# Four chained attention layers on one core: the counting and mean products are moved from ahead of the causal attention's first score products to behind them

## The reference

```
Q = relu(x @ Wq + bq); K = relu(ctx @ Wk + bk); V = relu(ctx @ Wv + bv)
key_masks = sign(abs(sum(K, axis=-1)))          # a key counts if its row of K isn't all zero
scores = where(key_masks == 0, NEG, Q_ K_^T / 4)
scores = where(tril == 0, NEG, scores)           # NEG = -2**32 + 1, not minus infinity
out = relu(softmax(scores) V_ @ Wo + bo) + x, then a norm over each row
```

## Time and profile before

| what | us |
|---|---|
| median of 3 runs | 1596.85 |
| the three runs | 1592.26, 1596.85, 6304.54 |
| the profiled execution, device time | 1590.74 |
| its span | 1588.9 |
| PE busy | 1426.6 (90%) |
| DVE busy | 864.6 (54%) |
| ACT busy | 716.6 (45%) |
| mean granted PE clock | 0.965 |

### The profile page before, as it was taken

The page is one execution under the profiler, slowest core; times in us unless marked ns, Lnnn a source line. Parts: engine busy times, 40 slices in busy tenths (PEclk is TensorE's granted clock), DMA queues, the critical chain, the costliest instruction groups (busy, mean ns, idle before and its releaser), DMA issues.

```text
span 1588.9 us, 23992 instructions
## 1 busy us (share of the span) xinstructions
PE 1426.6 (90%) x8204; PEld 713.9 (45%) x8232; DVE 864.6 (54%) x2099; ACT 716.6 (45%) x1177; POOL 263.6 (17%) x138
## 2 busy tenths in 40 slices
PE   5999898888999988888999998988899998988886
PEld 2336555423533654543443464553263355455334
DVE  2663565585266256567355536556636635655762
ACT  0663353455366234427446425352825632625462
POOL 1004131301100413220110213121011041303001
PEclk9999999989999989998999998998999999999898
DMA  9000404303200230540310031242031005043210
GB/s 339 22 1 12 102 1 91 70 14 113 68 1 7 38 70 1 99 75 1 126 55 1 8 62 45 38 86 51 1 127 54 1 8 106 2 71 64 41 60 14
DMA packets 44776, 85.28 MB, mean 54 GB/s; under 512 B 10464, under 2 KB 27872, under 8 KB 44384
## 3 DMA queue, kind: packets, MB, share of 16 engines
q1 hardware_dynamic: 41136, 73.17, 18.6%
q10 hardware_dynamic: 3504, 10.39, 3.2%
HBM read 43.68 MB, written 2.10 MB: 29 GB/s over the span
## 4 chain that ended last, share of the span: by engine, by line
PE 62%; DVE 15%; issue 10%; ACT 5%; SPq 3%; DMA 3%; ACTq 1%; POOL 0%; DVEq 0%; POOLq 0%
PE ring L1286 8%; PE obank L1296 8%; PE ring L1276 7%; DVE nmax L1075 7%; PE ring L1463 6%; PE ring L1252 6%; PE ring L1352 4%; PE ring L1603 3%; PE obank L1513 3%; PE ring L1201 3%; ACT q_all L771 3%; PE ring L1454 2%; SPq L413 2%; DVE rbuf L1094 2%; DMA q_all<-q_parts 1%
## 5 line engine op out<-in xcount | busy, mean ns | idle before, releaser
L1075 DVE TENSOR_REDUCE nmax<-ring 128x2 f32<-128x1024 f32 (+1 forms) x192 | 218.5, 1175 | 51.3 <-PE ring L1463 33.7
L679 ACT ACTIVATE region_e<-region_d,nmin 128x512 f32<-128x512 f32 x256 | 182.6, 714 | 83.7 <-DVE nmin L936 82.6
L936 DVE CUSTOM_DVE_ANT_0 region_d<-ring,maskb 128x512 f32<-128x512 f32 x256 | 165.9, 686 | 91.5 <-issue 89.4
L784 ACT ACTIVATE region_e<-ring 128x1024 f32<-128x1024 f32 x192 | 183.4, 992 | 55.7 <-PE ring L1463 32.7
L771 ACT ACTIVATE q_all<-ring 2x1024 fp32r<-2x1024 bf16 x96 | 97.6, 1016 | 204.7 <-PE ring L1524 204.2
L606 POOL TENSOR_TENSOR nat_x<-nat_n,rows 128x1024 f32<-128x1024 f32 x16 | 37.6, 2353 | 606.1 <-DVE nat_n L985 461.2
L1286 PE MATMUL ring<-region_q 64*128 64x512 f32 x512 | 126.9, 615 | 6.7 <-ACT region_q L668 5.4
L1454 PE MATMUL ring<-cbf 64*128 64x128 bf16 (+2 forms) x1280 | 131.7, 286 | 0.0
L1071 DVE TENSOR_REDUCE nmax<-ring 128x4 f32<-128x512 f32 (+1 forms) x96 | 86.1, 911 | 75.0 <-PE ring L1454 74.3
L1296 PE MATMUL obank<-region_e,vs 128*64 128x512 f32 x512 | 124.0, 605 | 0.0
L780 ACT ACTIVATE region_e<-ring 128x768 f32<-128x768 f32 (+1 forms) x96 | 74.0, 776 | 55.1 <-PE ring L1454 52.8
(11 more groups left out here) (193 smaller groups left out, 2171.4 us busy)
## 6 DMA issues: line engine op xcount, KB each, us to landing
q_all<-q_parts SPq DMA_DIRECT2D x192, 64.0 KB, 2.5
region_e<-in_w_f SPq DMA_DIRECT2D x8, 1024.0 KB, 5.8
k_tiles_a<-k_parts SPq DMA_DIRECT2D x96, 64.0 KB, 2.3
k_tiles_b<-k_parts SPq DMA_DIRECT2D x96, 64.0 KB, 2.3
q_all<-q_parts ACTq DMA_DIRECT2D x96, 64.0 KB, 3.2
wvo<-in_wv SPq DMA_DIRECT2D x5, 1024.0 KB, 5.1
wqk<-in_wq SPq DMA_DIRECT2D x4, 1024.0 KB, 9.1
wqk<-in_wk SPq DMA_DIRECT2D x4, 1024.0 KB, 11.1
```

Source lines behind the costliest of these rows:

```text
L679: ins = act.activation(e0[:, n % E0, h, :], sm0[:, n % 2, h, :], ACT.Exp, bias=nmin0[:, n, h:h + 1], scale=-1.0, accum_out=sum0[:, n, h:h ...
L784: act.activation(e16[:, n % 4, 2 * u:2 * u + 2, 0:nq], slot((a, "B", g, kt, u))[:, :, 0:nq], ACT.Exp)\
L936: ins = dve.tensor_tensor_reduce(out=sm0[:, n % 2, h, :], in0=slot(("S0", p, kt))[:, h, :], in1=maskb[:, :], scale=-1.0, scalar=3.0e38, op ...
L1075: dve.tensor_reduce(nmax[:, qt, 2 * u:2 * u + 2], slot(name)[:, :, 0:nk], AX.X, ALU.max, negate=True)\
```

## The change

The three jobs `cnt`, `meanV` and `meanO` leave the place ahead of `attention(CAUSAL)` and become steps of group 0, on PE, on DVE and in the list of jobs alike. `cnt` and `meanV` now stand behind the six A jobs of group 0 and ahead of A of group 1, tile 0; `meanO` stands behind T of group 0. The dummies ahead of the causal A jobs become 12 in place of 6, and the three behind them go. Nothing is computed otherwise.

```diff
 def group_steps(a, g):
     if g == 0:
-        steps += ahead(a, 1, 0) + ahead(a, 1, 1) + [("T", 0)] + ahead(a, 1, 2) + ahead(a, 1, 3)
+        steps += [("cnt",), ("meanV",)] if a == CAUSAL else []
+        steps += ahead(a, 1, 0) + ahead(a, 1, 1) + [("T", 0)] + ([("meanO",)] if a == CAUSAL else []) + ahead(a, 1, 2) + ahead(a, 1, 3)
...
-    jobs += [("X", 1), ("ksum",), ("Q2",), ("cnt",), ("meanV",), ("meanO",)]
+    jobs += [("X", 1), ("ksum",), ("Q2",)]
...
+                def degenerate_rows():
+                    dve.wait_ge(*filled_by(("cnt",), b))
+                    dve.tensor_scalar(degen[:, :], slot(("cnt",))[:, 0, 0:NT], 0.5, None, ALU.is_lt).then_inc(*ends_drain(("cnt",)))
...
+                            if kind == "cnt":
+                                degenerate_rows()
+                            if kind == "meanV":
+                                mean_of_values()
+                            if kind == "meanO":
+                                mean_output()
                 drain_q_relu(("Q2",), "bq2")
-                dve.wait_ge(*filled_by(("cnt",), b))
-                dve.tensor_scalar(degen[:, :], slot(("cnt",))[:, 0, 0:NT], 0.5, None, ALU.is_lt).then_inc(*ends_drain(("cnt",)))
...
-                dst = start(("cnt",))
-                pe.wait_ge(*drained_by(("ksum",), b))
...
                     if a == CAUSAL:
-                        keep_warm(6)
+                        keep_warm(12)
                     for qt in range(NT):
...
-                    keep_warm(3)
+                    if a != CAUSAL:
+                        keep_warm(3)
...
                         for kind, *which in group_steps(a, g):
-                            if kind in "ABTV":
+                            if kind == "cnt":
+                                count_keys()
+                            elif kind == "meanV":
+                                mean_values()
+                            elif kind == "meanO":
+                                mean_heads()
+                            elif kind in "ABTV":
```

More of the change, by code:

```diff
@@ L133, in attention_jobs @@
     for g in range(GROUPS):
-        jobs += [(a,) + step for step in group_steps(a, g) if step[0] in "ABT"]
+        jobs += [(a,) + step if len(step) > 1 else step for step in group_steps(a, g) if step[0] not in "VMH"]
     return jobs
@@ L1107, in head_out, with mean_of_values, mean_output @@
                     ins.then_inc(out_drained, 1)
+                def degenerate_rows():
+                    dve.wait_ge(*filled_by(("cnt",), b))
+                    dve.tensor_scalar(degen[:, :], slot(("cnt",))[:, 0, 0:NT], 0.5, None, ALU.is_lt).then_inc(*ends_drain(("cnt",)))
+                def mean_of_values():
+                    dve.wait_ge(*filled_by(("meanV",), b))
+                    dve.tensor_scalar(spread[:, :, :], slot(("meanV",))[:, 0, 0:DT].unsqueeze(2).broadcast_to([P, DT, P]), 1.0 / S, None, ALU.mult)\
+                        .then_inc(*ends_drain(("meanV",)))
+                def mean_output():
+                    dve.wait_ge(*filled_by(("meanO",), b))
+                    dve.tensor_copy(mean_o[:, :], slot(("meanO",))[:, 0, 0:D]).then_inc(*ends_drain(("meanO",)))
                 def attention(a):
@@ L1121, in attention @@
                                 head_out(a, *which)
-                drain_q_relu(("Q2",), "bq2")
-                dve.wait_ge(*filled_by(("cnt",), b))
-                dve.tensor_scalar(degen[:, :], slot(("cnt",))[:, 0, 0:NT], 0.5, None, ALU.is_lt).then_inc(*ends_drain(("cnt",)))
[L1127 to L1131, removed]
+                            if kind == "cnt":
[4 more added lines that the diff above has]
+                                mean_output()
+                drain_q_relu(("Q2",), "bq2")
                 attention(CAUSAL)
@@ L1540, in attention, with count_keys, mean_values, mean_heads @@
                         for kind, *which in group_steps(a, g):
-                            if kind in "ABTV":
-                                {"A": pass_a, "B": pass_b, "T": turn_maxima, "V": values}[kind](a, *which)
+                            if kind == "cnt":
[5 more added lines that the diff above has]
+                            elif kind in "ABTV":
+                                {"A": pass_a, "B": pass_b, "T": turn_maxima, "V": values}[kind](a, *which)
+                def count_keys():
+                    dst = start(("cnt",))
+                    pe.wait_ge(*drained_by(("ksum",), b))
+                    for qt in range(NT):
+                        for kt in range(qt + 1):
+                            ins = pe.matmul(dst[:, 0, qt:qt + 1], (tri if kt == qt else ones)[:, :], km[:, kt:kt + 1],
+                                            start=(kt == 0), stop=(kt == qt))
+                    ins.then_inc(*ends_fill(("cnt",)))
+                def mean_values():
+                    dst = start(("meanV",))
+                    pe.wait_ge(vmask_ready, (b + 1) * NT)
+                    for i in range(DT):
+                        for kt in range(NT):
+                            ins = pe.matmul(dst[:, 0, i:i + 1], v2[:, kt, i * P:(i + 1) * P], ones[:, 0:1], start=(kt == 0), stop=(kt == NT - 1))
+                    ins.then_inc(*ends_fill(("meanV",)))
+                def mean_heads():
+                    dst = start(("meanO",))
+                    pe.wait_ge(*drained_by(("meanV",), b))
+                    pe.wait_ge(k_loaded["om"], b * 16 + 16)
+                    for t in range(DT):
+                        ins = pe.matmul(dst[:, 0, 0:D], spread[:, t, :], w_om[:, t, :], start=(t == 0), stop=(t == DT - 1))
+                    ins.then_inc(*ends_fill(("meanO",)))
                 def out_heads(a, name):
```

## The result

The changed kernel takes 1607.4 us (median), the kernel before 1596.85 us. The ratio, taken over the fast runs alone and so without before's run of 6304.54 us, is 1.0077 with a 95% interval of 1.0059 to 1.0094; that is 12 us more, where the two medians differ by 10.5. It is slower, by more than the noise and by far less than 2%. The forecast of 1597 was 10 us too low, and the measured time lies 0.4 us beyond the upper end of the range. The profiled execution took 1608.33 us, 17.6 more than the one of before; before's was one of its fastest.

A forecast was written before the change was run, and what follows sets the result against it. PE was taken to bound the kernel, by when it can begin and what it waits for. Terms -9.9 + 8.4 + 1.2 + 6.0 - 2.0 = +3.7 us gave 1594.4, set at 1597 us with 3 us added; range 1586 to 1607.

The forecast's parts named there:

- Step 1: First A job of each batch: starts when its last DMA lands, not behind the moved products; 9.9 us faster in all.
- Step 2: From first A to first B job: the moved products lengthen 9.93 us to 12.0, 8.4 us slower in all.
- Step 3: Clock around the moved block: half clock costs 1.2 us at first A jobs, 6.0 in block; later fall gains 2.0.
- The sign that step 3 named: From first A to first B job: 12 to 14 us expected in the changed kernel's trace.
- The later end of step 3: From first B job to T of group 1: the clock's later fall is over earlier, 0.5 us less a batch, 2.0 in all.
- rival (b): The moved block: clock falls ahead of it, every product paid at 1.2 GHz; +14 us, 1607 us, chance 0.18.
- deciding point: Start of the count: each batch with the clock at half there adds up to 4.0 us.
- Rival (a): Block and B jobs: the moved products fill PE's idle gaps and keep 2.4 GHz; -7 us, 1587 us, chance 0.22.

The follow-up runs named there:

- e10: The changed kernel with 28 dummies ahead of the A jobs in place of 12, and each product of count and mean 64 columns wide: ratio 0.9977.
- e2: The kernel before with only the projection of the mean moved behind job T, dummies as before: ratio 0.9926, and 0.9946 when run again.
- e1: The changed kernel with 28 dummies ahead of the causal A jobs in place of 12: ratio 1.0041 to the kernel before.
- e5: The changed kernel with its count cut from ten products to one and its mean from eight to two: ratio 0.9982, 1593.5 us.

## Why the prediction was wrong

**Step 1 was right.** It gave 9.9 us for the earlier first A jobs. Measured between `ksum` and that job: 1.8, 3.1, 3.3 and 1.7 us, 9.9 in all. The DMA was the release, 0.06 us ahead.

**Step 2 was right, and only e10 could show it.** Count at +4.55, T at +9.15, first B job at +12.0, from rows at full clock. e10 has +4.32, +9.09 and +12.02. The 8.4 us that the block costs by its length stand. One term had a wrong row: the projection's 1.69 us in the earlier trace rows was taken partly at half clock; from its start to that of the next product it takes some 1.0 at full clock, and so ACT's copy, not PE, releases the first B job in e10. One reading on the way to this sum was off too: PE did not go without a break from the queries to the dummies, since the projection waited 0.50 us for DVE's spread (between 179.01 and 179.51; 0.52 in the earlier trace rows). That wait and the projection are what e2 takes off the path.

**Step 3 failed, in "That is 0 to 4.0 us a batch" and "I take 1.5, 6.0 in all".** Taking e10's 12.0 us away from the changed kernel's distances leaves 5.7, 4.1, 4.0 and 4.9 us, 18.7 in all, for the clock; the prediction had 7.2 (1.2 for the first A job and 6.0). In batch 0, against e10: A jobs to count 5.17 for 4.32, +0.85; count 4.28 for 2.28, +2.0; mean 3.49 for 1.88, +1.6; A job of group 1 1.07 for 0.61, +0.5; T to first B job 3.68 for 2.93, +0.75. The count, the mean and what follows are each somewhat over what the prediction gave as the bound, and the A jobs are well over the 0.3 us that it gave to the first of them. The bounds add up to 4.3 us a batch, and batch 0 measured 5.7. Worse was the choice inside the bound. It took the middle because before the change the clock fell 2.5 and 5.0 us behind the first one-column product. But there the queries' wide products stood ahead of them; in the new place the gap and the thin A jobs do, which is the likely reason for the earlier fall. So the clock was at half before the block began in batches 0 and 3, and it fell 1.6 and 1.8 us into it in the others. The sign that step 3 named, 12 to 14 us from first A to first B job, was passed in every batch (16.0 to 17.7).

The later end of step 3 was right in sign and near in size: from first B job to T of group 1 all batches take 7.03 us in place of 7.12 and 7.90, 2.7 us less for the 2.0 taken.

**The sum again**: -9.9 + 8.4 + 18.7 - 2.7 = +14.5 us, which is the stretch's 142.9 - 128.4, against +3.7 forecast; and 12 us timed. That is rival (b), priced at +14 and 1607 us, with a chance of 0.18. Its deciding point, the clock at the start of the count, was met in two batches; in the other two the mean, the T job and the projection were slow all the same. What spoke for it in the profile of before was the 3.25 us mean of batch 1; what I set against it, that the clock came back to full behind the same A jobs, was a misreading. By the earlier trace rows with the earlier trace rows the clock was back at about 183.4 and 569.1, ahead of the first A jobs at 183.55 and 569.68 and behind the projection and the dummies; the A jobs had not brought it back, they had only not brought it down. Rival (a), too, can be seen: e10 with its full clock has -9.7 for the first A jobs, +8.3 for the block and -5.5 from first B job to T of group 1, the terms by which (a) came to -7; its stretch is 6.8 us shorter than before's, and 4 us of that were timed.

The Trainium skill's rule against idle gaps between bursts (TensorE: Matmul & The Clock Gate, section Why this matters for your kernels) points the right way: the gap ahead of the A jobs costs about half of the loss, as e1 shows, and in the changed kernel, with its gap of 4 us, the clock was down in all four batches at the latest 0.9 us behind the start of the first A job. Taken alone it is not enough here: e1 has no gap of more than 0.7 us there and lost the clock in the count or the mean, with PE 100% busy by the profile from the count on.

What stays open are the few us by which profiled executions differ outside the stretch, and why e5 and e10 gained less in time than in their stretches. Where the clock falls is read from one profiled execution of each kernel, so from four batches. No width but 64 columns was tried.

## What to carry to other kernels

Work that hides behind a wait must stand where the wait is long and nobody behind it is late: here count and mean were free or nearly so under the DMAs' landing, while behind the A jobs they cost some 2 us a batch at full clock, about half of their length, and up to 7.8 with the clock at half. So moving only the projection, which itself waits for DVE, was right. When a stream of narrow products is moved, ask at which clock it will run and what it does to the clock of the work behind it; rows taken in the old place don't carry that over, since they hold the clock of their old neighbours. Where weight loads take up all the time of a stream of narrow products, as here (PEld 3.40 of 3.40 us in e1), try them wider: 64 columns were free to within the 0.02 us shown below, and held the clock.

## What the runs showed of the hardware

The clock fell to 1.2 GHz while the profile had PE and its weight loads busy without a break, with products of one moving column (e1: the fall at 190.7, inside 187.90 to 191.30 at PE 3.40 of 3.40 us, with thin A jobs ahead), and held at 2.4 GHz with the same number of products of 64 columns (e10, the same A jobs ahead, all four batches). The 64 columns cost next to nothing: the eight products of the mean (16 records) took 1.95 us in e10 and 1.93 us with one column at full clock in e2. At half clock the one-column products took 3.55 us in the changed kernel, nearly double.
